# Eight-wide attention heads: value products in pairs, maxima beside the crossed masks, the split of the maxima on ScalarE and GpSimd, masks loaded a unit earlier

## The reference

```python
# layer 2: slopes bias, integer mask, one extra term in the sum
scores = jnp.einsum('bhqd,bhkd->bhqk', Q, K) * scale - slopes * (query_pos - key_pos)
scores = jnp.where(mask[:, None, :, :] == 0, -jnp.inf, scores)
m = jnp.max(scores, axis=-1, keepdims=True)
e = jnp.exp(scores - m)
out = einsum(e / (1.0 + sum(e)), V) @ W_o.T
# layer 3: biases, two boolean masks, ordinary softmax, scale 128 ** -0.5
```

## Time and profile before

| | |
|---|---|
| median of 3 executions | 1727.19 us (1725.11 to 1728.86) |
| profiled execution | 1728.73 us, its span 1726.9 us |
| layer two's steps 1 to 8, in the span | 948.0 to 1203 us |
| layer three's steps 1 to 8, in the span | 1427.3 to 1680 us |
| TensorE, VectorE, ScalarE, GpSimd busy over the span | 81%, 64%, 45%, 38% |
| mean granted TensorE clock | 0.885 of 2.4 GHz |

### The profile page before, as it was taken

How to read it: one execution, slowest core, us unless ns; L and a number is a source line. 1 busy time by engine, 2 the same in 40 slices (tenths; PEclk the granted TensorE clock), 3 DMA queues, 4 the chain that set the end, 5 groups by cost and what they waited for, 6 DMA issues and landing times. The chain is left out here.

```text
span 1726.9 us, 30865 instructions
## 1 busy us (share of the span) xinstructions
PE 1401.9 (81%) x10350; PEld 764.1 (44%) x10350; DVE 1100.5 (64%) x3283; ACT 776.2 (45%) x1089; POOL 658.0 (38%) x425
## 2 busy tenths in 40 slices
PE   6999954705999999999335899999699759999992
PEld 4555443702666666666221333333466513333331
DVE  5888844145666676665585777773366678777735
ACT  3666620303666566654020555555233305555550
POOL 4666512261666676668521122110500062224000
PEclk9999985955999999999655999999699859999995
DMA  4545522433533333220024343220100042311100
GB/s 152 211 180 221 217 79 65 113 47 119 198 135 142 141 142 117 81 102 2 14 57 108 63 111 78 63 63 2 29 16 19 6 104 38 66 37 38 33 2 28
DMA packets 83933, 148.60 MB, mean 86 GB/s; under 512 B 18220, under 2 KB 55241, under 8 KB 80207
## 3 DMA queue, kind: packets, MB, share of 16 engines
q1 hardware_dynamic: 80264, 117.73, 23.6%
q10 hardware_dynamic: 1728, 25.17, 3.7%
q0 software_dynamic: 1808, 3.94, 1.2%
HBM read 99.95 MB, written 46.16 MB: 85 GB/s over the span
## 5 line engine op out<-in xcount | busy, mean ns | idle before, releaser
L1759 DVE CUSTOM_DVE_ANT_0 a_junk<-a_psM,a_madd 128x512 bf16<-128x512 f32 x512 | 331.9, 683 | 98.9 <-issue 95.9
L1705 ACT ACTIVATE a_probs<-a_psE 128x1024 f32<-128x1024 f32 x256 | 261.9, 1023 | 222.1 <-PE a_psE L1596 221.1
L2149 DVE TENSOR_REDUCE a_mx<-a_psM 128x1 f32<-128x512 f32 x256 | 161.0, 670 | 135.6 <-PE a_psM L1976 135.6
L1596 PE MATMUL a_psE<-a_maddT,res_identb 64*128 64x512 bf16 x1024 | 221.0, 388 | 2.1
L1573 PE MATMUL a_psM<-narrow_k_op,narrow_q_op 57*128 57x512 bf16 (+1 forms) x512 | 152.5, 415 | 57.7 <-DMA narrow_q_op<-a_qs 35.1
L176 POOL TENSOR_SCALAR res_xn<-res_X,res_mv,n_rstd 128x128 f32<-128x128 f32 x32 | 26.8, 847 | 399.4 <-DVE n_rstd L162 399.4
L2111 ACT ACTIVATE a_probs<-a_psE 128x1024 f32<-128x1024 f32 x128 | 130.8, 1024 | 86.0 <-PE a_psE L1996 82.6
L1949 POOL TENSOR_TENSOR a_half_sum<-a_probs 128x1024 f32<-128x1024 f32 x64 | 150.7, 2355 | 39.4 <-ACT a_probs L2111 39.2
L1607 PE MATMUL a_psO<-a_probs,narrow_values 128*32 128x256 f32 x2048 | 162.8, 392 | 2.7 <-ACT a_probs L1705 1.1
L1992 PE MATMUL a_psE<-a_qT,a_kT 64*128 64x256 f32 x1024 | 133.7, 381 | 0.0
L2008 PE MATMUL a_psO<-a_probs,a_values 128*64 128x256 f32 x1024 | 124.6, 385 | 0.8 <-ACT a_o_raw L2095 0.8
(11 more groups left out here) (317 smaller groups left out, 2633.4 us busy)
## 6 DMA issues: line engine op xcount, KB each, us to landing
wide_k<-a0a_k_stage SPq DMA_DIRECT2D x32, 512.0 KB, 2.6
wide_v<-a0a_v_stage SPq DMA_DIRECT2D x32, 512.0 KB, 4.3
a_k_part<-wide_k SPq DMA_DIRECT2D x64, 256.0 KB, 3.1
a_kT<-wide_k ACTq DMA_DIRECT2D x6, 2048.0 KB, 7.9
a_values<-wide_v ACTq DMA_DIRECT2D x6, 2048.0 KB, 8.4
keys<-a0a_parts SPq DMA_DIRECT2D x96, 64.0 KB, 2.0
narrow_k_op<-keys SPq DMA_DIRECT2D x32, 192.0 KB
f0e_w<-in_L_W SPq DMA_DIRECT2D x16, 256.0 KB
```

The costliest lines, as they stand in the source:

```text
L1596: return pe.matmul(psE[s % 2][:, j, :, :], res.identb[group, :], maddT[r][group, s % 2 * 2:s % 2 * 2 + 2, :], start=False, stop=last, skip ...
L1705: act.activation(probs[:, head:head + 2, k:k + 2, :], psE[s % 2][:], ACT.Exp).then_inc(exped, 1)
L1759: dve.tensor_tensor_reduce(junk[j][:], psM[j][:], madd[r][:, t, :], 1.0, -3.0e38, ALU.add, ALU.max, mx[r][:, max_place(h, t):max_place(h, ...
L2149: dve.tensor_reduce(mx[r][:, at:at + 1], psM[j][:], AX.X, ALU.max).then_inc(max_read, 1)
```

## The change

Value products: `products_of(s)` gives none in even half steps and two in odd ones, s - 5 and s - 4 (a negative number means the last four of the unit before). They now stand between the straight masks and the first maximum. The two maxima matmuls are no longer issued together: the first stands before the crossed mask of the other row group, the second before the other crossed mask. `turn_out` moves from half step 5 to 6 and `turn_back` from 7 to 8. `read_out` on ScalarE goes in front of the exponential of half step 3. The maxima are copied out of PSUM, negated, by ScalarE (`take_maxima`, after the exponential of half steps 10 and 1), and GpSimd cuts them into three parts in between its masks. SP loads the masks of unit v + 1 after the queries of unit v, and GpSimd makes two masks ahead instead of three. Two loops are written out.

```diff
-        MAX_SLOTS, READ_SLOT, OUT_SLOT, BACK_SLOT, PROJECT_SLOT, V_SLOT = (10, 1), 3, 5, 7, 9, 12
+        MAX_SLOTS, READ_SLOT, OUT_SLOT, BACK_SLOT, PROJECT_SLOT, V_SLOT = (10, 1), 3, 6, 8, 9, 12
+        LAG = READ_SLOT + 1
+        def products_of(s):
+            return (s - LAG - 1, s - LAG) if s % 2 else ()
 # SP
-                        load_masks(v, r)
-                        load_keys(v, r)
-                        load_queries(v, r)
+                    load_keys(v, r)
+                    load_queries(v, r)
+                    if v + 1 < B:
+                        sp.wait_ge(masked, 2 * (v - 1))
+                        load_masks(v + 1, (v + 1) % RING)
 # GpSimd
+                def split_max(v, half):
+                    done = (2 * v + half) * n_split
+                    neg, parts = neg_max[half], max_parts[half]
+                    if v > 0:
+                        pool.wait_ge(max_in[half], 96 * v)
+                    pool.wait_ge(max_out, 2 * v + half + 1)
+                    pool.tensor_copy(parts[:, 0, :], neg[:]).then_inc(max_split, 1)
+                    pool.wait_ge(max_split, done + 1)
+                    pool.tensor_tensor(max_rest[:], neg[:], parts[:, 0, :], ALU.subtract).then_inc(max_split, 1)
+                    pool.wait_ge(max_split, done + 2)
+                    pool.tensor_copy(parts[:, 1, :], max_rest[:]).then_inc(max_split, 1)
+                    pool.wait_ge(max_split, done + 3)
+                    pool.tensor_tensor(parts[:, 2, :], max_rest[:], parts[:, 1, :], ALU.subtract).then_inc(max_split, 1)
+                for u in range(2):
+                    masks(u, u, 0, True)
+                split_max(0, 0)
+                for v in range(1, B):
+                    split_max(v - 1, 1)
+                    if v + 1 < B:
+                        masks(v + 1, (v + 1) % RING, (v + 1) // RING, v + 1 < RING)
+                    split_max(v, 0)
+                split_max(B - 1, 1)
 # TensorE
+                        for i in products_of(s):
+                            if i >= 0 and take_exp:
+                                weigh(v - 1, before, i // QUAD, i % QUAD, first)
+                            if i < 0 and finish:
+                                weigh(v - 2, (r - 2) % RING, (HEADS + i) // QUAD, i % QUAD, False)
                         if take_max:
-                            for j in range(2):
-                                maximum(v, r, s, j, first and v == 0)
+                            maximum(v, r, s, 0, first and v == 0)
                         if take_exp:
                             pe.wait_ge(half_masked, (v - 1) * HEADS + s + 1)
-                            mask(before, s, 1, 0, True)
-                            mask(before, s, 0, 1, True).then_inc(scored, 1)
-                        (one weigh in every half step)
+                            mask(before, s, 0, 1, True)
+                        if take_max:
+                            maximum(v, r, s, 1, first and v == 0)
+                        if take_exp:
+                            mask(before, s, 1, 0, True).then_inc(scored, 1)
 # ScalarE
+                def take_maxima(v, half, first):
+                    if not first:
+                        act.wait_ge(max_split, (2 * (v - 1) + half + 1) * n_split)
+                    act.wait_ge(max_turned, 2 * v + half + 1)
+                    act.activation(neg_max[half][:], psX[0:HALF * QT, 0:P], ACT.Identity, scale=-1.0).then_inc(max_out, 1)
 # VectorE
-                def split_max(v, half):
-                    (four instructions on 16x128, after the maxima of half steps 1 and 10)
```

More of the change, by code:

```diff
@@ L1372, in narrow_attention @@
         mx = [ph.sb(f"mx{i}", [P, HEADS * QT]) for i in range(RING)]
+        neg_max = [ph.sb(f"neg_max{i}", [HALF * QT, P]) for i in range(2)]
         max_rest = ph.sb("max_rest", [HALF * QT, P])
@@ L1486, in _ @@
                 load_queries(1, 1)
+                load_masks(2, 2)
                 sp.wait_ge(stored[1], n_stores * (NCHUNK - 1))
@@ L1489, in _ @@
                 maxima(0, 0, 1)
[L1490 to L1493, removed]
-                        load_masks(v, r)
-                        load_keys(v, r)
-                        load_queries(v, r)
-                        maxima(v - 1, (r - 1) % RING, 0)
-                        maxima(v - 1, (r - 1) % RING, 1)
+                for v in range(2, B):
+                    r = v % RING
+                    sp.wait_ge(exped, (v - 2) * HEADS + 1)
+                    load_keys(v, r)
[3 more added lines that the diff above has]
+                        load_masks(v + 1, (v + 1) % RING)
+                    maxima(v - 1, (r - 1) % RING, 0)
+                    maxima(v - 1, (r - 1) % RING, 1)
                 maxima(B - 1, (B - 1) % RING, 0)
@@ L1521, in masks @@
                         last.then_inc(masked, 1)
-                for u in range(RING):
-                    masks(u, u, 0, True)
[L1525 to L1529, removed]
+                def split_max(v, half):
[12 more added lines that the diff above has]
+                for u in range(2):
+                    masks(u, u, 0, True)
+                split_max(0, 0)
[5 more added lines that the diff above has]
+                split_max(B - 1, 1)
             @block.tensor
@@ L1664, in _ @@
                 steps(pe, step)
-                for t in range(KT):
-                    weigh(B - 1, (B - 1) % RING, QUADS - 1, t, False)
+                for i in range(HEADS - LAG, HEADS):
+                    weigh(B - 1, (B - 1) % RING, i // QUAD, i % QUAD, False)
                 pe.wait_ge(added, B - 1)
@@ L1698, in step @@
                     for s in range(HEADS):
+                        if finish and s == READ_SLOT:
+                            read_out(v - 2)
                         if take_exp:
@@ L1705, in step @@
                             act.activation(probs[:, head:head + 2, k:k + 2, :], psE[s % 2][:], ACT.Exp).then_inc(exped, 1)
+                        if take_exp and s == MAX_SLOTS[1]:
+                            take_maxima(v - 1, 1, not inner and v == 1)
+                        if take_max and s == MAX_SLOTS[0]:
+                            take_maxima(v, 0, not inner and v == 0)
                         if finish:
-                            if s == READ_SLOT:
-                                read_out(v - 2)
                             if s == BACK_SLOT:
@@ L1785, in step @@
                             maximum(v, r, s)
-                        if take_exp and s == MAX_SLOTS[1]:
-                            if inner or v >= 2:
-                                dve.wait_ge(max_in[1], 96 * (v - 1))
-                            split_max(v - 1, 1)
                         if finish:
@@ L1794, in step @@
                                 add(v - 2)
-                        if take_max and s == MAX_SLOTS[0]:
-                            if inner or v >= 1:
-                                dve.wait_ge(max_in[0], 96 * v)
-                            split_max(v, 0)
                 steps(dve, step)
```

23 lines of the change are left out of this document (4 added, 19 removed).

## The result

The changed kernel took 1746.61 us (median of 11 runs, 1734.48 to 1752.77), the kernel before 1727.38 on the same chip (11 runs). The ratio is 1.0093, 95% interval 1.0075 to 1.0112: **slower by 0.9%**, where I had forecast no change and a range that ended at 1744. The profiled execution took 1746.30 us with a span of 1744.5, 17.6 more than before.

What follows compares the result with a forecast made beforehand. TensorE's queue, paused by VectorE's loop of maxima reads, was taken as the bound; -0.5 - 4.8 + 6 - 3.5 + 1.5 - 0.5 = -1.8 on the median 1727.19 gave 1725.4 us, range 1706 to 1744.

Steps and rivals of the forecast that it cites:

- the term of +6 (0 to +15): Layer two's maxima DMAs: split ready 1.25 us later, window from issue to use shrinks, about +1 for each of 7 steps.
- +1.5 for the first step: Layer two's first step: unit 2's masks are one more megabyte ahead of the maxima's DMAs; +1.5 us (0 to +5).
- my second rival: Six small maxima DMAs queue behind 1 MB of masks at each layer two step: +21 us, middle 1745; chance 0.20.
- VectorE's relief (-3.5): VectorE loses its splits, so delays of 0.72 + 0.87 and later reads and TensorE pauses go: -3.5 us (-1 to -5).
- first and last steps (-2.4): Each layer: step 1 gains 1 us from pairs without products, step 8, without maxima, gains 1.4 us.
- The plain pair: Two half steps without extra work take 3.56 us by VectorE's loop, 0.21 longer than before.
- Two products: Value products issued together cost TensorE 1.09 us against 1.32 for two apart, 0.23 less per pair of half steps.
- the third rival: Two products together keep both hand-overs: 0.14 more on the loop, +14 us, 1739; chance 0.05.
- The step without maxima: Step 8 of each layer: ScalarE bounds a pair of half steps at 3.05 us against 2 x 1.57.
- the first rival: VectorE's loop doesn't bind, so the 0.47 us pause in plain pairs goes: -39 us, 1686; chance 0.15.
- the full step: Whole steps come out even: 31.94 us against 32.02 in layer three, 30.91 against 30.90 in layer two.
- My sum for that layer: Layer three: -0.5 for full steps, -2.4 for first and last steps, -0.5 for one VectorE split less at its start.

Runs made afterwards that it cites:

- masks_behind: The changed kernel with the masks of unit v + 1 sent behind the first six maxima DMAs, no longer in front of them: 1723.47 us, ratio 0.9969.
- masks_none: The changed kernel without the mask loads of units 3 to 7, so no mask bytes stand in front of those units' maxima rows: 1735.2 us, ratio 0.9985.
- split_back: The changed kernel with the split of the maxima back on VectorE, in place of ScalarE and GpSimd: 1738.59 us, ratio 1.0066.
- single_behind: The changed kernel with masks behind the first maxima DMAs and one value product in every half step: 1708.25 us, ratio 0.9826; run again 0.9818.

## Why the prediction was wrong, step by step

**The step that failed** is the term of +6 (0 to +15) for layer two's transfers of maxima, worked out as a shrinking of the window between issue and need; with it went +1.5 for the first step. In place of +6 the waits rose by 10.3, and by 4.9 in place of +1.5 for the first (2.06 to 6.96); 6.5 more were lost at the lower clock behind them. Right were the parts of the delay: the split took 0.25 on ScalarE, then

```profile
1496.26 0.28 POOL L1538 CAST a_max_parts<-a_neg_max 16x128 bf16<-16x128 f32 x1 [6.70 <-ACT a_neg_max L1716]
1496.63 0.42 POOL L1540 TENSOR_TENSOR a_max_rest<-a_neg_max,a_max_parts 16x128 f32<-16x128 f32 x1
1497.11 0.28 POOL L1542 CAST a_max_parts<-a_max_rest 16x128 bf16<-16x128 f32 x1
1497.47 0.42 POOL L1544 TENSOR_TENSOR a_max_parts<-a_max_rest,a_max_parts 16x128 bf16<-16x128 f32 x1
```

1.63 us to 1497.89 (I took 1.8), with the rows issued 4.35 after the scores of s = 10 (I took 4.5). Wrong was to treat the landing as a fixed time from issue. I dismissed the masks' new place because the bytes in all were unchanged; what counts is which loads are still on their way when the rows are issued. This was my second rival, with a middle of 1745, and `masks_behind` and `masks_none` show it. That its 1745 comes so near to 1746.61 is partly luck: I had priced 21 us of waits, and it was 15.2 of waits and 6.5 of low clock. I also wrote that my range took in this middle, though it ended at 1744.

**A term left out** belongs to it. Behind a long wait TensorE runs at its lower level, 1.2 GHz, for some microseconds: the granted clock was 0.51 of full speed from 1020.9 to 1026.8 and 0.50 from 1058.2 to 1064.2, and 1.00 in the same half steps of layer three (1505.3 to 1509.2). Products in the changed kernel behind the wait at 1058.17, against 1.07 for the same elsewhere:

```profile
1061.09 1.93 PE L1632 MATMUL a_psO<-a_probs,narrow_values 128*32 128x256 f32 x16
```

The half steps 0 and 1 take 3.87 at full clock (1505.34 to 1509.21 in layer three). Behind the last five waits they took 5.41, 5.96, 6.06, 4.82 and 4.93: 7.8 us more. Behind the first wait, of 6.96, hardly anything is added: there the clock had been low from 900 to 904 on in both kernels, and TensorE had been idle for some 20 us before the layer's first maxima. Before, only those at 982.07, behind the wait of 4.08, were long in that way (4.84 against 3.55); waits of 0.77 and 2.02 had no such mark. But 2.06 in `masks_behind` and 2.22 in `split_back` had one, so near 2 us it goes either way. The Trainium skill (TensorE: Matmul & The Clock Gate, HAM oscillation) says that a stream which stops for its transfers can fall back at each stop; the 1.93 us and the granted clock of 0.50 agree.

Layer two then adds up as: waits +15.2, low clock 7.8 - 1.3 = +6.5, hand-overs (below) +3; that is 24.7 against +18.8 measured. The other -5.9 is the size of my terms for VectorE's relief (-3.5) and this layer's first and last steps (-2.4). No run takes these apart, but the traces do, by the starts of the scores. VectorE's late splits had made half step 12 of before longer in four steps, by 4.4 in all; in the changed kernel it is the same 2.77 in every step. One of the four holds the subtraction of 1.15 in the earlier trace rows, which I had priced at 0.87. It cost 2.8, and 1.5 of that at the lower clock that followed TensorE's stop (granted 0.50 from 1105.7 to 1109.1):

```profile
1104.01 0.39 PE L1573 MATMUL a_psM<-narrow_k_op,narrow_q_op 57*128 57x512 bf16 x1 [1.25 <-DVE a_mx L1759]
...
1105.73 2.08 PE L1661 MATMUL a_psX<-narrow_wv,a_cT 128*128 128x128 f32 x8
```

The same projection took 1.16 at full clock. Step 0 got 1.5 shorter beside its wait, the last stretch from step 8 on 1.0, step 1 got 0.4 longer, and 0.6 is left.

**Steps that held.** The plain pair: 3.56, to 0.01. Two products: 1.07 busy, one hand-over between masks and them; the third rival falls. The step without maxima: half steps of 1.77 and 1.28 at the end of layer three (1690.57 to 1692.34 to 1693.62), 3.05 as worked out. No table load was added on ScalarE (two at the line of the exponentials in both kernels). No plain pair took 3.1, so the first rival falls for this layout; `single_behind` shows what a pause less is worth.

**A small error in the full step.** I had 31.94 for layer three; it took 32.47 (1476.74 to 1509.21). A piece of the reason is in the turn-out, PE's timeline:

```profile
1517.39 0.39 PE L1621 MATMUL a_psE<-a_maddT,res_identb 64*128 64x512 bf16 x1
1517.71 0.66 PE L1572 MATMUL a_psX<-res_ident,a_OT 128*128 128x128 f32 x4
1518.30 0.39 PE L1615 MATMUL a_psE<-narrow_q_op,narrow_k_op 51*128 51x256 bf16 x4
```

The turn starts 0.32 behind the last mask, not 0.22. Before, the float32 products stood there and had paid that hand-over; now each piece of float32 work behind bf16 masks pays 0.10 itself. The pairs with turn-out and turn-back took 4.25 and 4.03 (I had 4.15 and 3.93), the one with the projection 5.17 (4.97), the one with the value projection 4.76 (4.65). In all, with what rounding leaves, 0.53 a step, 3.2 us in layer three's six. My sum for that layer was -0.5 - 2.4 - 0.5; with +3.2 it is -0.2, and +2.3 was measured. The remaining 2.5 us are in the first and last steps: step 1 took 30.68 us against 29.48 before, where I had taken -1 for it, and from step 8 on 0.4 was gained, not 1.4 (0.7 went the other way elsewhere). What makes step 1 longer wasn't tried; its half steps 1 and 2 took 4.50 together and 3 and 4 took 3.17, where I had taken about 2.5 for each of these pairs.

## What to carry to other kernels

In this kernel a small transfer landed when the loads still under way in front of it let it: when loads change places in a queue, look at what stands between the last big load and each small urgent one, not at the sum. And look at what waits behind the small one in the same queue: here the next unit's loads did. Price a new wait of TensorE as the wait and the slow stretch behind it. Where two loops meet, spread the shared work evenly over the half steps: one product in each beat two in every second by 0.43 a pair (3.13 against 3.56), though the second product alone is cheap.

## What was not expected of the hardware

The scores behind six transfers of 2 KB, issued 3.5 us behind a megabyte of masks, started 11.4 us after the first of them was issued, and in six steps 1.2 to 1.4 us after the second mask had landed. Sending the rows 1.1 us earlier into a backlog moved nothing in the one step looked at. The price of going from bf16 masks to float32 work, 0.10 us, falls on whichever float32 matmul comes first. The fastest kernel of the study, one product in each half step with masks behind the rows, runs at 0.982 of the kernel before.
